# State-space mixer on one Trainium2 core: the scaling of the next piece's state product changes places with an accumulation on VectorE

## The reference, cut to what matters

```python
scores = einsum('bclhn,bcshn->bhcls', C_c, B_c)
Y_diag = einsum('bhcls,bcshp->bclhp', scores * Lmat, xdt)
states = einsum('bcshn,bhcs,bcshp->bchpn', B_c, decay_states, xdt)
def step(carry, inp):                     # over the pieces of a sequence
    s, d = inp
    return (carry * d[:, :, None, None] + s, carry)
Y_off = einsum('bclhn,bchpn,bhcl->bclhp', C_c, prev_states, state_decay)
y = (Y_diag + Y_off) + D * x
g = y * silu(gate)                        # then normalised per group and multiplied by W_out
```

## Time and profile before

| | us |
|---|---|
| median of 3 runs | 2422.06 (2418.85 to 2424.81) |
| the profiled execution | 2423.18 |
| its span | 2421.4 |
| mixer loop within it, about | 245 to 1612 |

### The profile page before, as it was taken

One profiled execution on the slowest core, in us unless ns is written; L12 is line 12 of the kernel. 1 busy time (PEld: TensorE's weight loads), 2 busy tenths in 40 slices (PEclk: granted clock), 3 DMA queues, 4 the chain that ended last, 5 costly groups with the idle time before them and its releaser, 6 DMA issues. The chain is left out here.

```text
span 2421.4 us, 38962 instructions
## 1 busy us (share of the span) xinstructions
PE 2188.3 (90%) x12970; PEld 1687.8 (70%) x12970; DVE 1834.8 (76%) x3270; ACT 1153.8 (48%) x2419; POOL 1228.3 (51%) x1323
## 2 busy tenths in 40 slices
PE   4995899999999999999999999988977998899972
PEld 3784688888888888888888888867766776344432
DVE  4885788888888888888888888855663444888745
ACT  1332455555555555555555555533342333466660
POOL 3543366566565664665665655544333333999000
PEclk9998699999999999999999999998988999899996
DMA  2002000000000000000000000025115555333214
GB/s 94 1 14 76 32 3 3 33 3 2 33 3 33 3 3 33 3 3 33 3 3 34 3 3 3 3 106 191 46 53 132 177 177 145 107 121 119 76 62 159
DMA packets 76886, 128.89 MB, mean 53 GB/s; under 512 B 22331, under 2 KB 54683, under 8 KB 74683
## 3 DMA queue, kind: packets, MB, share of 16 engines
q1 hardware_dynamic: 69827, 107.65, 13.1%
q0 software_dynamic: 6864, 18.75, 3.2%
HBM read 91.82 MB, written 46.92 MB: 57 GB/s over the span
## 5 line engine op out<-in xcount | busy, mean ns | idle before, releaser
L957 DVE SCALAR_TENSOR_TENSOR mix_cv<-mix_pp,mix_cw,mix_cv 128x384 f32<-128x384 f32 (+4 forms) x864 | 492.7, 570 | 25.4 <-ACT mix_cv L880 4.5
L804 PEld LDWEIGHTS mix_pyd<-mix_xdt,mix_lm 128*128 128x128 f32 x2048 | 248.1, 192 | 56.6 <-issue 53.1
L880 ACT ACTIVATE mix_cv<-mix_pp,mix_cb,mix_cw 128x384 f32<-128x384 f32 (+1 forms) x288 | 182.4, 633 | 204.9 <-PE mix_pp L80 204.9
L78 PE MATMUL mix_pp<-l0in_XH,mix_wx_lo 128*128 128x384 f32 (+2 forms) x576 | 239.1, 415 | 40.5 <-DVE mix_ss L946 25.4
L743 POOL TENSOR_TENSOR mix_xdt<-mix_xtok,l_dt 128x512 f32<-128x512 f32 x128 | 133.8, 1045 | 277.3 <-ACT mix_xtok L907 277.3
L736 POOL TENSOR_TENSOR mix_t<-mix_t,mix_xd 128x512 f32<-128x512 f32 x112 | 144.5, 1290 | 218.8 <-DVE mix_t L971 153.3
L855 PE MATMUL mix_pgt<-mix_wo,mix_gt 128*128 128x256 f32 x1024 | 244.9, 382 | 2.9 <-issue 2.2
L804 PE MATMUL mix_pyd<-mix_xdt,mix_lm 128*128 128x64 f32 x2048 | 243.4, 272 | 2.5 <-DVE mix_lm L1007 2.5
L1915 DVE TENSOR_REDUCE att_tops<-att_psc 128x1 f32<-128x512 f32 (+3 forms) x384 | 189.6, 549 | 46.7 <-PE att_psc L1863 32.2
L886 ACT ACTIVATE mix_pp<-mix_cv 128x384 f32<-128x384 f32 (+1 forms) x288 | 133.0, 462 | 161.8 <-DVE mix_cv L957 159.1
L855 PEld LDWEIGHTS mix_pgt<-mix_wo,mix_gt 128*128 128x128 f32 x1024 | 184.1, 190 | 31.2 <-issue 9.2
(11 more groups left out here) (388 smaller groups left out, 5808.7 us busy)
## 6 DMA issues: line engine op xcount, KB each, us to landing
mix_w_raw<-in_w_in SPq DMA_DIRECT2D x8, 1280.0 KB
y_d<-exp_ys SPq DMA_DIRECT2D x79, 128.0 KB, 1.7
a_part<-att_sums SPq DMA_DIRECT2D x32, 256.0 KB, 5.1
mix_ll<-cs SPq DMA_DIRECT2D x384, 4.0 KB
q<-q SPq DMA_DIRECT2D x12, 512.0 KB, 4.5
k<-k SPq DMA_DIRECT2D x12, 512.0 KB, 4.8
att_qs<-q SPq DMA_DIRECT2D x32, 192.0 KB
att_ks<-k SPq DMA_DIRECT2D x32, 192.0 KB
```

The costliest lines, as they stand in the source:

```text
L78: pe.matmul(out, l_lo, r_hi, start=start, stop=False)
L804: last = pe.matmul(pyd[:, h * HP:(h + 1) * HP], lm[p % 2][:, h, :], xdt[p % 2][:, h * HP:(h + 1) * HP], start=True, stop=True)
L880: act.activation(conv_tile(k), pp[k % 2][:, halo:cols], ACT.Identity, bias=cb[:, it // 2, ct:ct + 1], scale=cw[:, it // 2, ct, 3:4]).then_ ...
L957: last = dve.scalar_tensor_tensor(out, of, cw[:, g, ct, 3 - d:4 - d], out, ALU.mult, ALU.add)
```

## The change

In slot c VectorE's list ended with the accumulation of piece c - 2, and slot c + 1 began with the scaling for piece c (there called p). The scaling now stands in slot c, directly ahead of the accumulation. It is the same instruction, with the same wait and the same signal. No other engine's list is touched.

```diff
@@ block.vector, in the loop over slots
-                    if 0 <= p < NC and p % CPS:
-                        dve.wait_ge(yo_done, n_off(p))
-                        dve.tensor_tensor(by_head(t1[o]), by_head(pyos), heads(TE1, p), ALU.mult).then_inc(t1_done, 1)
                     if len(fills(c - 1)) > 1:
                         finish(fills(c - 1)[-1])
...
                     if len(ks) > 1:
                         taps(ks[-1])
+                    n = c
+                    if 0 <= n < NC and n % CPS:
+                        dve.wait_ge(yo_done, n_off(n))
+                        dve.tensor_tensor(by_head(t1[n % 2]), by_head(pyos), heads(TE1, n), ALU.mult).then_inc(t1_done, 1)
                     if 0 <= e < NC:
                         dve.wait_ge(op_done, e + 1)
```

## The result

The changed kernel took 2407.87 us (median of 6 runs, 2404.84 to 2409.42), the kernel before 2422.18 us in the same comparison. The ratio is 0.9937, with a 95% interval of 0.9926 to 0.9947: 14.3 us, or 0.6%, faster. (The ratio and its interval are an estimate over all runs; the quotient of the two medians is 0.9941.

The account below looks back on a forecast made before the run. TensorE was taken to set the pace nearly everywhere, gains coming only where it waits. 0.14 + 0.21 + 0.13 + 0.39 = 0.87 us per eight pieces, times 15 = 13.1 us, gave 2409 us; range 2401 to 2418.

Parts of the forecast that it names:

- The advance of 0.39 us at each y: VectorE's output sum y (L982) after a scaling can start 0.39 us earlier, as GpSimd's addition before it does.
- The scaling does not wait for L797: VectorE's moved scaling finds TensorE's product L797 ready, its modelled end 0.21 us before; if not, the gain is nil.
- The upper end of my bound: L797's product is there at its modelled end, so the scaling starts 0.39 us earlier and the summed gain holds.
- The four places: Slots after sums y of pieces 2, 3, 6, 7 modulo 8, where TensorE waits; together 0.87 us per eight pieces.
- After y(2): Slot after the sum of pieces 2, 10, 18 and so on: ScalarE's first tap L880 caps the gain at 0.14 us.
- after y(3): Slot after the sum of pieces 3 modulo 8: TensorE's short waits for ScalarE and product L990 vanish; gain 0.21 us.
- after y(6): Slot after the sum of pieces 6 modulo 8: ScalarE's first tap L880 caps the gain at 0.13 us.
- after y(7): Slot after the sum of pieces 7 modulo 8: TensorE's wait for exponential L916 shrinks by the whole advance; gain 0.39 us.
- The places that I priced at nothing: Slots after sums of pieces 0, 1, 4, 5 modulo 8, and the last pieces without block products; gain 0.
- TensorE sets the pace everywhere: Rival: TensorE bounds the whole loop and nothing changes, 2422 us; chance 0.17 together with the form where L797 is late.
- the caps do not hold: Rival: ScalarE's tap L880 also comes earlier and each place gives its 0.39 us; 20.7 us gain, 2402; chance 0.12.
- The late accumulation: Rival: the accumulation, ending 0.60 us later, holds up TensorE's next gate product L78; 18 us slower, 2441; chance 0.05.

Follow-up runs that it names:

- S = (1, 4, 5): The swap made only for pieces with p % 8 = 1, 4 or 5, the order of before elsewhere; 2422.28 us, ratio to before 0.9998.
- partial kernels: Four kernels swapping only pieces with p % 8 = 7; 1, 4, 5; 2, 6; or 3, else as before: 2414.84, 2422.28, 2417.74, 2421.5 us.
- S = (3,): The swap made only for pieces with p % 8 = 3, the order of before elsewhere; 2421.5 us, ratio to before 0.9991.

## Why the prediction was right

**The advance of 0.39 us at each y** held: the idle time before y fell by 0.41 in the rows of y(2) (1.07 to 0.66), and S = (1, 4, 5) shows 0.39 for each of its 48 pieces on average.

**The scaling does not wait for L797.** This was the open step, since the ends of matmuls are modelled. VectorE waits for L797 in 4 pieces only, as before (5.5 us in place of 3.3, because in these last pieces the accumulation no longer stands ahead of the wait). The upper end of my bound was the right one.

**The four places.** After y(2) 0.14 was forecast and 0.14 measured; after y(3) 0.21 and 0.22; after y(6) 0.13 and 0.14; after y(7) 0.39 and 0.38. After y(7) the price was right with half of the reason: the prediction names the wait for L916 alone, and the kernel that makes the exponential first shows that VectorE's product with the gate holds TensorE at the same place just as long. The 0.39 came through because both start from y(7); when the wait for L916 alone was taken away, the pattern gained 0.01. The partial kernels give the same: 0.26 for the first and third together, 0.21, and 0.38. The places that I priced at nothing gave nothing.

**The rivals.** That TensorE sets the pace everywhere is refuted by the interval of the result. The Trainium skill (Perfetto Trace Analysis, Identifying the Most-Contended Engine) says to optimize the engine with the highest occupancy first, and to judge TensorE by its weight loads and its share of the peak rate, not by the busy share of its matmuls. By weight loads TensorE stands at 70% of the span and VectorE at 76%, so the busy share of the matmuls, on which this rival rests, is not the one that the page goes by. Nor does VectorE's share alone price the change: 43.8 us of its idle time went, and 14.3 us of the total. The same page's Optimization Strategy, to look for the gaps on the engine in question and for what ends them, fits what the traces show: half of the slots gave nothing, and the gain sat in TensorE's gaps. That the caps do not hold is refuted by the taps' new waits for L880. The late accumulation did no harm, but for a reason that has a size: 0.48 us of room in the slot of y(7), as worked out. One place further back the room is used up there and in the slot before y(0), which took the whole gain back.

**What was off.** The prediction counts five of eight slots in which TensorE has no such wait; its own walk has four. It reads the row of L964 in the earlier trace rows (37.5 us, 32 times) as waits of a third block product. By the timeline 9 of the 32 stand ahead of the first piece (246 to 272 us), 8 after y(2) and 15 after y(6); in the other patterns the wait after y(2) has no name. Of TensorE's total waits it expected 4 us less for L964 and about 7 less for L916; they fell by 2.1 and 8.8. The first is 15 times 0.13 and 7 times 0.14, 2.9 us, less 0.8 by which one wait ahead of the first piece was longer (1.29 and 2.07). The places themselves are as forecast. In the experiments the prices of waits that feed back into the loop were too small: 2 us a pattern expected and 2.97 measured with the scaling ahead of the taps, 130 us expected and some 183 measured with the accumulation behind y (2591.4 against 2407.9). In both I followed the delay along TensorE's queue and not on to what ScalarE and VectorE then waited for.

## What to carry to other kernels

Where one engine is busy nearly all the time, list its own waits and what ends each, and price a change on another engine place by place: in this kernel the gain at each place was the least of the advance, of the next input's room, and of the wait that was there to be won. Look for a second wait right behind the first, and for waits to which the profile gives no name: here both took part. Of 43.8 us of idle time taken from VectorE here 14.3 came through, and the walk through four places said so beforehand. When an instruction is put back to let another one go first, measure the room to whoever waits for it, in every kind of slot: here it was 0.48 us in one place, and one more step back cost 12 us by the patterns and 15 by the medians.

## What the runs showed that I had not expected

The first pattern of the loop is not as steady as the others. In the profiles of the changed kernel y of piece 9 starts at 377.95 in one and at 377.26 in the other, at 378.10 and 376.64 in two of the partial kernels, and at 374.01 where ScalarE's exponential goes first, though the steady patterns agree to 0.01 us between repeats. The traces show what goes with it: TensorE's granted clock in the first slots, the number behind the five busy times. From 278 to 290 us, in the kernel before, in the changed kernel and in the one with the exponential first:

```profile
core 0: us, PE busy (x) PEld busy (x) DVE busy (x) ACT busy (x) POOL busy (x), PEclk, DMA share, GB/s
278.00:290.00 12.00, 9.94 (x53) 8.12 (x53) 8.86 (x14) 5.79 (x13) 3.58 (x5) 0.86 0.01 2
...
278.00:290.00 12.00, 10.06 (x50) 8.85 (x49) 7.70 (x13) 4.26 (x9) 2.12 (x3) 0.72 0.01 2
...
278.00:290.00 12.00, 10.21 (x70) 8.44 (x70) 10.75 (x19) 6.15 (x14) 5.64 (x7) 1.00 0.01 3
```

In all three the clock was at its lower level (0.50) from 250 to 270 us, while TensorE was busy for 7.2 to 7.7 of every 10 us; in the steady loop it is 1.00. From y of piece 0 to y of piece 1 it took 11.0 us, 11.5 us and 9.5 us in these three, and 12.3 in the changed kernel's repeat, whose clock was 0.72 too. So the early y of piece 9 in the last kernel is the clock's doing in that one execution; whether its edit has a part in it was not tried.

A larger part of the differences between profiled spans lies behind the mixer's loop. From y of piece 127 to the end of the span it took 814.8 us before, 812.0 and 812.4 in the two profiles of the changed kernel, and 808.9 in the kernel with S = (3,), whose edit does not touch that part. What sets this was not tried. Both are reasons why the length of the pattern told more than the span.
